# The first half's condition step in two quarters, loads in the order of need, and four engine orders rewritten, in a one-core attention and feed-forward kernel

## The chip, the cores and the metric

The kernel runs on one core of a Trainium2 chip. The metric is device time in microseconds (us) of one execution. The kernel before takes 228.81 us (median of three runs, 228.77 to 230.34). A core has TensorE (PE in the profile, PEld its weight loads), VectorE (DVE), ScalarE (ACT), GpSimd (POOL) and SyncE (SP), each with its own instruction stream; they meet at semaphores only. DMA transfers are issued here from SP and ACT.

## What is computed

`x` is 32 batches x 32 tokens x 256 features. The reference, cut to what matters:

```python
w = cond_weights[itok]                       # (B, 32, 32), one of 8 tables for each batch
c = einsum('bct,bcd->bdt', x, w) + fside[itok][:, :, None]       # the condition step
q, k, v = split(c @ W_qkv + b_qkv)           # 16 heads of 16, causal, scale 1/16
x = x + (softmax(q k^T / 16) v) @ W_out + b_out
g = silu(lora(x, Wg, Ag, Bg)) * lora(x, Wu, Au, Bu)    # adapters Ag[itok], Bg[itok], ...
y = lora(g, Wd, Ad, Bd)
x = x + fwht(silu(y @ W1.T) * (y @ W3.T)) @ W2.T       # Walsh-Hadamard over 1024
```

Products that need it are exact to fp32 by splitting: each operand is hi (rounded to the fast fp32r format) plus lo (the rest), and three matmuls hi*hi, lo*hi, hi*lo are added in PSUM.

## The kernel before, in words

The 1024 tokens are worked in two halves of 512 (s = 0, 1; 16 batches each). 128 feature rows make a chunk c or m. Every engine's order of work is written out by hand as a list of calls, and the PSUM bank of every early tile stands in the table `EARLY_BANKS`.

- **Condition step.** DVE turns the batch indices into one-hots (`index_f`, L866; `onehot_slot`, L869; `onehot_n`, L872). For each half it then multiplies the eight tables by the one-hot (`condition_product`, L877, 1024 elements per partition, written over spare room in `k_x`), adds over the eight (`condition_sum`, L883) and spreads the result block-diagonally over four batches (`condition_blocks`, L889, written over spare room in `prob`). PE multiplies `x_slot` (it lies in `k_x` too) with these blocks, four groups a half and chunk, each of one matmul that the profile shows as two (`conditioned`, L404), and adds the bias rows (`conditioned_bias`, L411), which DVE made (`condition_bias`, L899). The bank `xc` then holds the input of q, k and v.
- ACT rounds it to `act_hi` (`conditioned_hi`, L664), DVE subtracts to get `act_lo` (`conditioned_lo`, L911), and PE forms q, k (`projected`, six matmuls of 512 columns each, L385, L387, L389), v (twelve of 256 columns, L440 to L442), scores (a causal tile, L450, and 64 small matmuls, L460), values (64 small ones, L485), then the output projection, the adapters, gate and up.
- **Softmax, a tile of 512 at a time** (four tiles a half): DVE `maxima`, `less_maxima`; ACT `exps`; DVE `sums`, `inverses`; POOL `normalised` (L1159); DVE `turn` (transpose); ACT `spread_slots`; POOL `spread_first` (L1165). `values(s, 0)` needs tiles 0 and 1, `values(s, 1)` tiles 2 and 3.
- **Weights** come as 25 batches (W_Q, W_K, W_V, W_OUT, W_A, W_GU ...) through a raw buffer of three places. ACT rounds each (`split_weights`, L659), DVE (the first three) or POOL (L1134) makes the rest (`weights_lo`). SP may load a batch into a place only when the batch three earlier has been split.
- `w2_t` (1 MB) lands in `tmp_b`; its four parts are split by ACT (`fold_raw_hi`, L745) and POOL, and PE applies part of the Hadamard transform to it (`fold`, L469).
- At the start PE runs 14 matmuls on zeros (L533).

The order around the change: SP issues const, W_Q, W_K, W_V, matrices, `w2_t`, the residual input (`x_feat`, 1 MB) and then W_OUT and so on. ACT issues the index and the two halves of `x_slots`. PE does the condition step of both halves before anything else.

Of the kernel before, what the change touches and what calls it, by code (L numbers as in the profile page):

```python
# [37 lines left out]
ALU = mybir.AluOpType  # L38
ACT = mybir.ActivationFunctionType
AX = mybir.AxisListType  # L40

P = 128
# [50 lines left out]
def ring_places():  # L93
# [38 lines left out]
def psum_tiles():  # L132
# [7 lines left out]
    plan += [(name, (5, 4, 6, 3, 1, 7, 2, 0)[n % 8]) for n, name in enumerate(later)]  # L140
# [29 lines left out]
def build(nc, index, first, x_slots, w_stream, matrices, w2_t, x_feat, out):  # L170
    with ExitStack() as ctx:
# [10 lines left out]
        index_f = sb("index_f", [P, NG + B])  # L182
# [54 lines left out]
        idx_slot = index_f[:, 0:NG]  # L237
        idx_row = index_f[:, NG:NG + B]
# [103 lines left out]
        def _(sp):  # L342
# [23 lines left out]
        def _(pe):  # L366
# [175 lines left out]
            query(0, 0)  # L542
            key(0, 0)
            fold(0)
            key(0, 1)
            query(0, 1)
            scores(0, 0)
            key(1, 0)
            scores(0, 1)
            query(1, 0)  # L550
            key(1, 1)
            v(0, 0)
            scores(1, 0)
            fold(1)
            v(0, 1)
            query(1, 1)
            values(0, 0)
            v(1, 0)
            scores(1, 1)
            values(0, 1)  # L560
            fold(2)
            project(0, 0, 0, 1)
            v(1, 1)
            project(0, 1, 0)
            project(0, 1, 1)
            fold(3)
            values(1, 0)
            adapters_in(0, 0, 0, 1)
            adapters_in(0, 1, 0)
            gate_up(0, 0)  # L570
# [6 lines left out]
            gate_up_adapters(2, 0)  # L577
            project(1, 0, 0, 1)
            gate_up(3, 0)
            project(1, 1, 0)  # L580
            gate_up_adapters(3, 0)
            project(1, 1, 1)
            gate_up(4, 0)
# [65 lines left out]
        def _(act):  # L649
# [101 lines left out]
            fold_raw_hi(0, 1, 2)  # L751
            conditioned_hi(0, 1)
            fold_raw_hi(3)
            conditioned_hi(1, 0)
            split_weights(W_V)
            conditioned_hi(1, 1)
            split_weights(W_OUT)
            queries(0, 0)
            keys(0, 0, 0, 1)
            evacuate_fold(0)  # L760
            keys(0, 1, 0, 1)
            split_weights(W_A)
            queries(0, 1)
            split_weights(W_GU)
            exps(0, 0)
            keys(1, 0, 0, 1)
            exps(0, 1)
            keys(1, 0, 2, 3)
            exps(0, 2)
            queries(1, 0)  # L770
            keys(1, 1, 0, 1)
            spread_slots(0, 0)
            exps(0, 3)
            evacuate_v(0, 0)
            spread_slots(0, 1)
            keys(1, 1, 2, 3)
            evacuate_v(0, 1)
            spread_slots(0, 2)
            evacuate_fold(1)
            exps(1, 0)  # L780
            even_heads(0, 0)
            queries(1, 1)
            even_heads(0, 1)
            spread_slots(0, 3)
            exps(1, 1)
            attention_hi(0, 0)
            evacuate_v(1, 0)
            spread_slots(1, 0)
            even_heads(0, 2, 3)
            evacuate_fold(2)  # L790
            attention_hi(0, 1)
            spread_slots(1, 1)
# [530 lines left out]
```

## Time and profile before

| | |
|---|---|
| median of 3 runs | 228.81 us (228.77 to 230.34) |
| the profiled execution | 228.75 us, its span 227.0 us |
| busy PE / PEld | 221.5 us (98%) / 179.7 us (79%) |
| busy DVE / ACT / POOL | 84.8 / 100.8 / 121.2 us |
| granted PE clock | full in every slice |
| chain of work that ended last | PE 94%, DVE 3%, DMA 1% |

The span runs from the first instruction to the last; 1.75 us of the execution's own time lie outside it. Matmuls are pipelined, so their busy times overlap and the step from one start to the next tells what one costs.

### The profile page before, as it was taken

To read this page: it belongs to the slowest core of one execution; us is meant where nothing else is said; L and a number is where in the kernel's file an instruction comes from. 1 tells how busy PE (TensorE), PEld (TensorE's weight loads), DVE (VectorE), ACT (ScalarE), POOL (GpSimd) and SP (SyncE) were. 2 spreads that over 40 slices of the span, in tenths; PEclk is the share of its full clock that TensorE was granted. 3 is DMA by queue.
4 is the path that set the end of the run, shared out by engine and by line. 5 is a ranking of instruction groups with operands and counts; after the bars stand their busy time and mean duration, and the time that the engine had idled before them with its cause. 6 is when DMAs were issued, how large, how long until landed. Compare 5 with 4: busy or idle time off the path is not lost.

```text
span 227.0 us, 3701 instructions
## 1 busy us (share of the span) xinstructions
PE 221.5 (98%) x1482; PEld 179.7 (79%) x1482; DVE 84.8 (37%) x141; ACT 100.8 (44%) x169; POOL 121.2 (53%) x93
## 2 busy tenths in 40 slices
PE   7799999999999999999999999999999999999995
PEld 2477787878788888888888888888888888888894
DVE  4988988888454342211022000202222222220211
ACT  2389798895853414756143000313355555440000
POOL 1029676637787297999993800180266667443000
PEclk9999999999999999999999999999999999999999
DMA  6956400004024100330110000031101100000211
GB/s 180 411 212 183 141 1 4 4 3 133 5 72 108 56 0 1 92 92 26 46 46 0 0 3 0 0 92 47 46 3 51 43 0 0 4 0 0 79 62 46
DMA packets 5345, 13.02 MB, mean 57 GB/s; under 512 B 720, under 2 KB 1360, under 8 KB 5072
## 3 DMA queue, kind: packets, MB, share of 16 engines
q1 hardware_dynamic: 4896, 11.72, 16.4%
q10 hardware_dynamic: 432, 1.07, 1.4%
q8 instruction: 12, 0.20, 0.4%
q14 instruction: 5, 0.04, 0.1%
HBM read 11.73 MB, written 1.05 MB: 56 GB/s over the span
## 4 chain that ended last, share of the span: by engine, by line
PE 94%; DVE 3%; DMA 1%; issue 0%; DVEq 0%
PE bank L385 28%; PE bank L389 28%; PE bank L387 28%; PE bank L460 3%; PE bank L485 2%; DMA index_i<-index 1%; DVE cond_sel L883 1%; DVE k_x L877 1%; PE bank L440 1%; PE bank L404 1%; PE bank L441 1%; PE bank L442 1%; PE bank L450 1%; PE bank L469 1%; PE bank L411 0%
## 5 line engine op out<-in xcount | busy, mean ns | idle before, releaser
L1172 POOL TENSOR_TENSOR h_lo<-tmp_b,h_hi 128x512 fp32r<-128x512 f32 x32 | 40.8, 1290 | 30.5 <-ACT h_hi L724 26.3
L385 PE MATMUL bank<-act_hi,w_hi 128*128 128x512 f32 x152 | 52.8, 392 | 0.1
L389 PE MATMUL bank<-act_hi,w_lo 128*128 128x512 f32 x152 | 52.4, 389 | 0.0
L387 PE MATMUL bank<-act_lo,w_hi 128*128 128x512 f32 x152 | 52.3, 389 | 0.0
L1018 DVE TENSOR_TENSOR tmp_b<-bank,tmp_a 128x512 f32<-128x512 f32 x32 | 21.1, 688 | 73.6 <-PE bank L389 56.2
L1134 POOL TENSOR_TENSOR w_lo<-raw,w_hi 128x512 fp32r<-128x512 f32 (+3 forms) x22 | 35.3, 1616 | 10.5 <-ACT w_hi L659 10.5
L385 PEld LDWEIGHTS bank<-act_hi,w_hi 128*128 128x128 f32 x152 | 28.5, 188 | 7.1 <-issue 1.1
L389 PEld LDWEIGHTS bank<-act_hi,w_lo 128*128 128x128 f32 x152 | 28.5, 188 | 6.0
L387 PEld LDWEIGHTS bank<-act_lo,w_hi 128*128 128x128 f32 x152 | 28.5, 188 | 5.7
L724 ACT ACTIVATE h_hi<-tmp_b 128x512 fp32r<-128x512 f32 x32 | 19.8, 632 | 28.4 <-DVE tmp_b L1018 28.4
L385 PE MATMUL bank<-h_hi,w_hi 128*128 128x512 f32 (+1 forms) x88 | 27.3, 370 | 0.0
L389 PE MATMUL bank<-h_hi,w_lo 128*128 128x512 f32 (+1 forms) x88 | 27.3, 370 | 0.0
L387 PE MATMUL bank<-h_lo,w_hi 128*128 128x512 f32 (+1 forms) x88 | 27.3, 370 | 0.0
L734 ACT ACTIVATE tmp_a<-bank 128x512 f32<-128x512 f32 x32 | 18.0, 595 | 20.7 <-PE bank L389 20.7
L659 ACT ACTIVATE w_hi<-raw 128x512 fp32r<-128x512 f32 (+3 forms) x25 | 18.1, 733 | 5.3 <-DMA raw<-w_stream 5.3
L385 PEld LDWEIGHTS bank<-h_hi,w_hi 128*128 128x128 f32 x88 | 16.6, 188 | 2.9
L387 PEld LDWEIGHTS bank<-h_lo,w_hi 128*128 128x128 f32 x88 | 16.6, 188 | 2.8
L389 PEld LDWEIGHTS bank<-h_hi,w_lo 128*128 128x128 f32 x88 | 16.6, 188 | 2.8
L385 PE MATMUL bank<-aux_hi,w_hi 128*128 128x512 f32 x44 | 16.3, 393 | 0.0
L387 PE MATMUL bank<-aux_lo,w_hi 128*128 128x512 f32 x44 | 16.2, 390 | 0.0
L389 PE MATMUL bank<-aux_hi,w_lo 128*128 128x512 f32 x44 | 16.2, 390 | 0.0
L1153 POOL TENSOR_TENSOR w_fold<-w_fold 128x1024 f32<-128x1024 f32 x6 | 15.3, 2561 | 0.0
(85 smaller groups left out, 246.1 us busy)
## 6 DMA issues: line engine op xcount, KB each, us to landing
raw<-w_stream SPq DMA_DIRECT2D x13, 256.0 KB, 2.7
raw<-w_stream SPq DMA_DIRECT2D x8, 384.0 KB, 3.2
raw<-w_stream SPq DMA_DIRECT2D x3, 512.0 KB, 3.6
k_x<-x_slots ACTq DMA_DIRECT2D x2, 512.0 KB, 6.7
tmp_b<-w_t SPq DMA_DIRECT2D x1, 1024.0 KB, 9.0
resid<-x_feat SPq DMA_DIRECT2D x1, 1024.0 KB, 10.9
out_feat<-tmp_b SPq DMA_DIRECT2D x3, 256.0 KB, 2.1
out_feat<-tmp_b SPq DMA_DIRECT2D x2, 128.0 KB, 1.8
```

The source lines that it names most:

```text
L385: pe.matmul(ps[:, :], w[0], x_hi, start=start, stop=False)
L387: pe.matmul(ps[:, :], w[0], x_lo, start=False, stop=False)
L389: last.append(pe.matmul(ps[:, :], w[1], x_hi, start=False, stop=stop))
L460: last = pe.matmul(tiles[i][32 * j:32 * j + 32, g * 4 * T:(g + 1) * 4 * T], q_t[s][q, c, b * T:(b + 1) * T], k_x[s][q, c, b], start=False, ...
L485: last = pe.matmul(o, v_tok[s][rows_, g, c * P + 32 * i:c * P + 32 * i + 32], prob_t[s][rows_, QUADS * c + i // 2, at:at + 2].rearrange("p ...
L659: act.activation(w_hi[:, at:at + COLS[n]], raw[:, n % STAGES, 0:COLS[n]], ACT.Copy)\
L724: act.activation(dst, tmp_b[:, ORDINAL[name, s, m] % 4, :], ACT.Copy).then_inc(prod_hi_made, 1)
L734: free(act.activation(tmp_a[:, n % 4, :], tile(name, s, m)[:, :], ACT.Silu), name, s, m)
L1018: free(dve.tensor_tensor(tmp_b[:, ORDINAL[name, s, m] % 4, :], tile(name, s, m)[:, :], tmp_a[:, silus % 4, :], ALU.mult), name, s, m)
L1134: pool.tensor_tensor(w_lo[:, at:at + COLS[n]], raw[:, n % STAGES, 0:COLS[n]], f32(w_hi[:, at:at + COLS[n]]), ALU.subtract).then_inc(w_lo_m ...
L1153: pool.tensor_tensor(b[:, t], a[:, 0], a[:, 1], ALU.subtract if t else ALU.add)\
L1172: pool.tensor_tensor(lo, tmp_b[:, n % 4, :], f32(hi), ALU.subtract).then_inc(prod_split, 1)
```

## The change

Half 0's condition step is done in two quarters of two groups each: DVE makes product, sum and blocks of each quarter, and PE may start on the first quarter's blocks (`conditioned` now does two groups for half 0, `conditioned_rest` the others). The cast of all 40 indices to fp32 is gone: `onehot_slot` compares the int32 index as it landed, and only the 32 indices of `idx_row` are cast, after it. SP waits for half 0 of `x_slots` before it issues W_V and the matrices, and for half 1 before `w2_t` and the residual input. Half 1's condition step moves behind half 0's q, k and first scores. `k_bias` moves ahead (`key_bias`). The lists of all four engines and the bank table are rewritten to fit. No matmul is added or taken away.

```diff
@@ sync
-            for n in range(STAGES):
-                load_weights(n)
+            load_weights(W_Q)
+            load_weights(W_K)
+            sp.wait_ge(x_loaded[0], 16)
+            load_weights(W_V)
             sp.dma_start(matrix[:, :], matrices).then_inc(matrix_loaded, 16)
+            sp.wait_ge(x_loaded[1], 16)
             sp.dma_start(tmp_b[:, :, :], w2_t.rearrange("p (j n) -> p j n", j=4)).then_inc(w2_loaded, 16)
@@ tensor
             def conditioned(s, c):
                 ps = claim("xc", s, c)
-                pe.wait_ge(blk_made, s + 1)
+                pe.wait_ge(blk_made, 3 if s else 1)
                 pe.wait_ge(x_loaded[s], 16)
-                for g in range(GROUPS):
+                for g in range(GROUPS if s else GROUPS // 2):
...
+            def conditioned_rest(s, c):
+                pe.wait_ge(blk_made, 2)
+                for g in range(GROUPS // 2, GROUPS):
+                    pe.matmul(tile("xc", s, c)[:, g * P:(g + 1) * P], x_slot[s][:, g, c * P:(c + 1) * P],
+                              cond_blk[:, s * GROUPS + g], start=False, stop=False, skip_group_check=True)
...
             conditioned(0, 0)
+            conditioned(0, 1)
+            conditioned_rest(0, 0)
+            conditioned_rest(0, 1)
             conditioned_bias(0, 0)
-            conditioned(0, 1)
             conditioned_bias(0, 1)
+            key(0, 0)
+            query(0, 0)
+            key(0, 1)
+            query(0, 1)
+            scores(0, 0)
             conditioned(1, 0)
+            fold(0)
             conditioned(1, 1)
...
@@ vector
-            dve.tensor_copy(index_f[:, :], index_i[:, :]).then_inc(setup, 1)
             dve.wait_ge(const_loaded, 16)
-            dve.wait_ge(setup, 1)
-            dve.tensor_tensor(onehot_slot[:, :, :], idx_slot.unsqueeze(2).to_broadcast([P, NG, N]),
+            dve.tensor_tensor(onehot_slot[:, :, :], index_i[:, 0:NG].unsqueeze(2).to_broadcast([P, NG, N]),
                               const[:, C_NROW:C_NROW + N].unsqueeze(1).to_broadcast([P, NG, N]),
                               ALU.is_equal).then_inc(setup, 1)
...
+            dve.tensor_copy(idx_row, index_i[:, NG:NG + B]).then_inc(setup, 1)
...
-            condition_product(0)
-            condition_sum(0)
-            condition_blocks(0)
+            condition_product(0, 0)
+            batch_onehots()
+            condition_sum(0, 0)
+            condition_product(0, 1)
+            condition_blocks(0, 0)
+            condition_sum(0, 1)
+            condition_blocks(0, 1)
             condition_bias(0)
```

How the rows stand on the engines that matter. On DVE at the start (`k_x` here is the product, `prob` the blocks, `w_hi` and `w_lo` of 8 partitions the bias rows), before:

```order
L866 CAST index_f<-index_i 128x40
L869 TENSOR_TENSOR onehot_slot<-index_f,const 128x64
L872 TENSOR_SCALAR onehot_n<-index_f,const 128x32
L877 TENSOR_TENSOR k_x<-const,onehot_slot 128x1024
L883 TENSOR_REDUCE cond_sel<-k_x 128x128
L889 TENSOR_TENSOR prob<-cond_sel,const 128x512
L899 TENSOR_TENSOR w_hi<-onehot_n,fs_hi 8x512
L899 TENSOR_TENSOR w_lo<-onehot_n,fs_lo 8x512
L877 TENSOR_TENSOR k_x<-const,onehot_slot 128x1024
```

and with the change:

```order
L874 TENSOR_TENSOR onehot_slot<-index_i,const 128x64
L877 CAST idx_row<-index_i 128x32
L891 TENSOR_TENSOR k_x<-const,onehot_slot 128x512
L881 TENSOR_SCALAR onehot_n<-idx_row,const 128x32
L899 TENSOR_REDUCE cond_sel<-k_x 128x64
L891 TENSOR_TENSOR k_x<-const,onehot_slot 128x512
L906 TENSOR_TENSOR prob<-cond_sel,const 128x256
L899 TENSOR_REDUCE cond_sel<-k_x 128x64
L906 TENSOR_TENSOR prob<-cond_sel,const 128x256
L916 TENSOR_TENSOR w_hi<-onehot_n,fs_hi 8x512
L916 TENSOR_TENSOR w_lo<-onehot_n,fs_lo 8x512
L923 TENSOR_TENSOR w_lo<-raw,w_hi 128x512 x2
```

The first blocks come after half-size steps, and the rest of W_Q and W_K now comes before half 1's product instead of after half 1's whole step.

On ACT from the first weight split on, with the change (`w_hi<-tmp_b` is a part of `w2_t`, the `w_hi<-raw` between the two `q_t` rows is W_OUT, the next one W_A):

```order
L668 ACTIVATE w_hi<-raw 128x512 x2
L673 ACTIVATE act_hi<-bank 128x512 x2
L668 ACTIVATE w_hi<-raw 128x512
L684 ACTIVATE k_x<-bank,k_bias,const 128x16x32 x2
L754 ACTIVATE w_hi<-tmp_b 128x512 x2
L677 ACTIVATE q_t<-bank,const 128x512
L668 ACTIVATE w_hi<-raw 128x512
L677 ACTIVATE q_t<-bank,const 128x512
L754 ACTIVATE w_hi<-tmp_b 128x512
L668 ACTIVATE w_hi<-raw 128x512
L754 ACTIVATE w_hi<-tmp_b 128x512
L684 ACTIVATE k_x<-bank,k_bias,const 128x16x32 x2
```

W_OUT, W_A and all of `w2_t` now stand ahead of half 0's second keys, which `scores(0, 1)` needs.

On POOL, the softmax of half 0 (`prob` is `normalised`, `k_x` is `spread_first`), before:

```order
L1134 TENSOR_TENSOR w_lo<-raw,w_hi 128x768
L1159 TENSOR_TENSOR prob<-prob,row_inv 128x512 x3
L1165 TENSOR_TENSOR k_x<-k_x,const 128x16x32
L1159 TENSOR_TENSOR prob<-prob,row_inv 128x512
L1165 TENSOR_TENSOR k_x<-k_x,const 128x16x32 x2
L1159 TENSOR_TENSOR prob<-prob,row_inv 128x512
L1165 TENSOR_TENSOR k_x<-k_x,const 128x16x32
```

and with the change:

```order
L1155 TENSOR_TENSOR w_lo<-raw,w_hi 128x768
L1180 TENSOR_TENSOR prob<-prob,row_inv 128x512 x4
L1186 TENSOR_TENSOR k_x<-k_x,const 128x16x32 x4
L1180 TENSOR_TENSOR prob<-prob,row_inv 128x512 x2
L1155 TENSOR_TENSOR w_lo<-raw,w_hi 128x768
```

All eight steps of half 0 now stand together, ahead of half 1's first.

## Rows read from the trace of the kernel before

**Rows 1.** The page: busy time (us, share, instructions).

```profile
PE 221.5 (98%) x1482; PEld 179.7 (79%) x1482; DVE 84.8 (37%) x141; ACT 100.8 (44%) x169; POOL 121.2 (53%) x93
```

**Rows 2.** Waits of PE after the warm-up (us in total, times, longest).

```profile
PE bank L404 <- DVE prob L889: 1.4, 2, 0.8
```

**Rows 3.** The chain that ended last, 0 to 48.3 us (start, us, what).

```profile
0.74 2.65 DMA index_i<-index
3.41 0.20 DVE index_f L866
...
3.71 0.23 DVE onehot_slot L869
3.93 0.15 DVE onehot_n L872
4.08 1.14 DVE k_x L877
5.25 1.23 DVE cond_sel L883
...
11.55 2.05 PE bank L404 x16
13.61 1.12 PE bank L411 x4
14.73 0.43 PE bank L385
...
18.17 0.23 PE bank L385
...
21.34 1.49 PE bank L460 x64
...
48.18 0.10 issue
```

**Rows 4.** Timeline (start, us, what; in brackets the idle time before and its releaser).

```profile
1.19 5.26 PE L533 MATMUL bank<-warm 128*128 128x512 bf16 x14 [1.19 <-DVE warm L864]
6.50 0.69 DVE L889 TENSOR_TENSOR prob<-cond_sel,const 128x512 f32<-128x512 f32 x1
7.11 0.67 DVE L899 TENSOR_TENSOR w_hi<-onehot_n,fs_hi 8x512 fp32r<-8x512 f32 x1
7.71 0.67 DVE L899 TENSOR_TENSOR w_lo<-onehot_n,fs_lo 8x512 fp32r<-8x512 f32 x1
7.25 1.16 PE L404 MATMUL bank<-prob,k_x 128*128 128x128 f32 x8 [0.79 <-DVE prob L889]
```

**Rows 5.** Timeline at 14 to 15.5 us: how ACT, DVE and PE hand over.

```profile
14.00 0.57 ACT L664 ACTIVATE act_hi<-bank 128x512 fp32r<-128x512 f32 x1
14.61 0.69 DVE L911 TENSOR_TENSOR act_lo<-bank,act_hi 128x512 fp32r<-128x512 f32 x1 [0.71 <-ACT act_hi L664]
15.35 0.19 PEld L385 LDWEIGHTS bank<-act_hi,w_hi 128*128 128x128 f32 x1 [0.16 <-DVE act_lo L911]
```

**Rows 6.** Loads: their issue in the timeline, and us to landing.

```profile
1.16 0.95 ACTq L652 DMA_DIRECT2D k_x<-x_slots  x2
DMA to landing us min/median/max: 5.9/6.7/7.5
resid<-x_feat SPq DMA_DIRECT2D x1, 1024.0 KB, 10.9
8.48 0.63 ACT L659 ACTIVATE w_hi<-raw 128x512 fp32r<-128x512 f32 x1 [1.71 <-DMA raw<-w_stream]
13.32 12.30 SPq L348 DMA_DIRECT2D raw<-w_stream  x6
```

**Rows 7.** Timeline: `scores(0, 1)` on PE, the last `spread_first` of half 0, and `values(0, 1)`.

```profile
24.80 1.56 PE L460 MATMUL bank<-k_x,q_t 64*32 64x128 f32 x64
39.37 1.04 POOL L1165 TENSOR_TENSOR k_x<-k_x,const 128x512 f32<-128x512 f32 x1 [0.18 <-ACT k_x L697]
40.61 1.15 PE L485 MATMUL bank<-k_x,v_tok 64*32 64x128 f32 x64
```

More of the change, by code:

```diff
@@ L139, in psum_tiles @@
     later += [("w2", j, 0) for j in range(len(OUTS))]
-    plan += [(name, (5, 4, 6, 3, 1, 7, 2, 0)[n % 8]) for n, name in enumerate(later)]
+    plan += [(name, (4, 2, 3, 1, 7, 6, 5, 0)[n % 8]) for n, name in enumerate(later)]
     held = [0] * 8
@@ L541, in _ @@
             conditioned_bias(1, 1)
[L542 to L547, printed above, removed]
+            scores(0, 1)
             key(1, 0)
-            scores(0, 1)
             query(1, 0)
+            v(0, 0)
             key(1, 1)
-            v(0, 0)
+            v(0, 1)
             scores(1, 0)
+            v(1, 0)
+            values(0, 0)
             fold(1)
-            v(0, 1)
+            values(0, 1)
             query(1, 1)
-            values(0, 0)
-            v(1, 0)
-            scores(1, 1)
[L560 to L566, printed above, removed]
+            v(1, 1)
+            project(0, 0, 0, 1)
+            fold(2)
+            project(0, 1, 0)
+            fold(3)
+            project(0, 1, 1)
+            scores(1, 1)
+            adapters_in(0, 0, 0, 1)
+            gate_up(0, 0)
+            adapters_in(0, 1, 0)
             values(1, 0)
-            adapters_in(0, 0, 0, 1)
-            adapters_in(0, 1, 0)
-            gate_up(0, 0)
             adapters_in(0, 1, 1)
@@ L750, in _ @@
             conditioned_hi(0, 0)
-            fold_raw_hi(0, 1, 2)
             conditioned_hi(0, 1)
+            split_weights(W_V)
+            keys(0, 0, 0, 1)
+            fold_raw_hi(0, 1)
+            queries(0, 0)
+            split_weights(W_OUT)
+            queries(0, 1)
+            fold_raw_hi(2)
+            split_weights(W_A)
             fold_raw_hi(3)
+            keys(0, 1, 0, 1)
+            exps(0, 0)
+            evacuate_fold(0)
             conditioned_hi(1, 0)
-            split_weights(W_V)
@@ L756, in _ @@
             conditioned_hi(1, 1)
[L757 to L763, printed above, removed]
+            exps(0, 1)
             split_weights(W_GU)
-            exps(0, 0)
             keys(1, 0, 0, 1)
-            exps(0, 1)
+            exps(0, 2)
             keys(1, 0, 2, 3)
-            exps(0, 2)
+            exps(0, 3)
             queries(1, 0)
+            spread_slots(0, 0)
@@ L785, in _ @@
-            exps(1, 1)
-            attention_hi(0, 0)
+            exps(1, 1)
+            even_heads(0, 1)
+            evacuate_fold(1)
+            even_heads(0, 2, 3)
+            attention_hi(0, 0)
+            queries(1, 1)
+            attention_hi(0, 1)
+            keys(1, 1, 2, 3)
+            split_weights(W_GU + 1)
+            evacuate_fold(2)
+            evacuate_fold(3)
+            residual_hi(0, 0)
+            split_weights(W_GU + 2)
+            residual_hi(0, 1)
+            spread_slots(1, 0)
@@ new lines, in groups, with condition_product @@
+            def groups(s, quarter):
+                half_ = GROUPS // 2
+                return range(GROUPS) if quarter is None else range(quarter * half_, (quarter + 1) * half_)
+            def condition_product(s, quarter=None):
+                gs = groups(s, quarter)
+                dve.wait_ge(setup, 1)
+                dve.tensor_tensor(cond_prod[s][:, gs.start:gs.stop],
+                                  cond_all.unsqueeze(1).to_broadcast([P, len(gs), T, N]),
+                                  onehot_slot[:, s * GROUPS + gs.start:s * GROUPS + gs.stop, :].unsqueeze(2)
+                                  .to_broadcast([P, len(gs), T, N]), ALU.mult).then_inc(prod_cond, 1)
@@ new lines, in condition_sum, with condition_blocks @@
+            def condition_sum(s, quarter=None):
+                gs = groups(s, quarter)
+                dve.wait_ge(prod_cond, 3 if s else quarter + 1)
+                dve.tensor_reduce(cond_sel[:, s * GROUPS + gs.start:s * GROUPS + gs.stop],
+                                  cond_prod[s][:, gs.start:gs.stop], AX.X, ALU.add).then_inc(sel_made, 1)
+            def condition_blocks(s, quarter=None):
+                gs = groups(s, quarter)
+                g = slice(s * GROUPS + gs.start, s * GROUPS + gs.stop)
+                dve.wait_ge(sel_made, 3 if s else quarter + 1)
@@ L1028, in _ @@
+            conditioned_lo(0, 1)
             condition_product(1)
+            key_bias()
+            condition_bias(1)
+            constants()
+            keys(0, 0, 2, 3)
             condition_sum(1)
             condition_blocks(1)
-            condition_bias(1)
-            weights_lo(W_Q)
-            conditioned_lo(0, 0)
-            conditioned_lo(0, 1)
-            weights_lo(W_K)
-            constants()
             weights_lo(W_V)
+            maxima(0, 0, 1)
+            less_maxima(0, 0)
```

159 lines of the change are left out of this document (63 added, 96 removed), and 24 rows, old and new, of the table EARLY_BANKS.

## The prediction

> **What bounds the kernel now.** I read the page's busy times first: PE is busy 98% of the span [rows 1], so only time in which PE stands idle or does needless work can be won. The waits view says where it stands: after the warm-up PE waits for one thing, the blocks of the condition step, twice and 1.4 us in all [rows 2], and for nothing else in the whole execution, apart from a break of 0.10 us at 48.18 [rows 3]. The chain of waits shows the same start: the index lands at 3.39, then comes an unbroken run of DVE steps (cast, one-hots, product, sum, blocks, bias rows, and the same again for half 1), and from 11.55 on the chain is PE alone [rows 3]. So the whole stake lies before 11.55. The timeline prices it. PE's first useful matmul starts at 7.25 [rows 4]. One half's condition work is 2.05 + 1.12 = 3.17 us of PE (16 and 4 matmul records, [rows 3]); half 0's would end at 7.25 + 3.17 = 10.42 and half 1's blocks come at 11.55, so 1.13 us are lost after the start. The warm-up ends at 1.19 + 5.26 = 6.45 [rows 4]; it is unchanged, and nothing useful can precede it. The most that can be won is therefore (7.25 - 6.45) + 1.13 + 0.10 = 2.0 us, or 0.9% of 228.75. A change of this kernel under 1% is what I call "the same".
>
> **The first blocks.** Before, they are ready at 6.50 + 0.69 = 7.19 [rows 4]. With the change the one-hot starts when the index has landed, 3.41, as the cast did. I have no row of a compare on int32; I take the fp32 row's 0.23 [rows 3] (bounds: the same row, or the cast's 0.20 on top, 0.43). The cast of 32 indices costs 0.15, between nothing and the 0.20 of the cast of 40. Halves of 1024-element steps: two steps of 512 start 0.60 apart (7.11, 7.71 [rows 4]), and a full one takes 1.14 to 1.23 [rows 3], so splitting costs nothing where steps follow without a dependence, and up to the 0.07 between 0.60 and 0.67 where one waits for the one before. So: product from 3.80, `onehot_n` 0.15, sum of the first quarter at 4.56 (it waits for its product), product of the second to 5.77, then blocks of 256 elements; their row is missing, between 0.35 (half the 0.69) and 0.69, I take 0.42: ready at **6.20**. The second quarter's blocks: 5.77 + 0.35 + 0.70 + 0.42 = 7.26. The bias rows follow, 0.60 and 0.67: 8.46, against 8.38 before [rows 4]. The saving of the first blocks is 1.0 us. A rule speaks against the split: the Trainium skill, "VectorE: DVE Perf Modes", section on the trn2 errata, says that each instruction on SBUF data pays a fixed latency and advises tiles of at least 512 elements; three more instructions at about 150 cycles of 0.96 GHz would put the bias rows at about 8.9, an estimate by that page. That would still change nothing in the sum below, but it would take about 0.3 us off the gain of the first rival.
>
> **But `x_slots` also has to be there.** Half 0's transfer is issued at 1.16 and takes 5.9 us: it lands at 7.06 [rows 6], hidden before behind blocks of 7.19. It now ends the wait: PE starts at about **7.1**, not 6.45. Whether it comes sooner when SP holds W_V back is the main doubt. W_K lands at about 8.45 (ACT's split starts at 8.48 after waiting for it [rows 6]), later than `x_slots`, and W_V stands behind W_K on SP's queue, so I take no gain; the bound is all that the warm-up allows, 0.6 us. The Trainium skill, "DMA: Bandwidth & Descriptors", section "Queues, rings and completion order", says that each DMA engine consumes one ring's descriptors in order and alternates between rings; by it W_V took next to nothing from `x_slots` before 7.06, and the sum is the one with no gain.
>
> From 7.1 the four quarters (two chunks each) are the same 16 records, 2.05: 9.16, later than the 8.46 of the bias rows and with both quarters' blocks long there. The bias for both chunks is 1.12: 10.28. Then PE has nothing to cover the hand-over, where before it had half 1. Chunk 0's bias ends at about 9.9; ACT starts `act_hi` at 9.93, DVE follows 0.61 later and PE 0.74 after that (14.00, 14.61, 15.35 [rows 5]): the first key starts at 9.93 + 0.61 + 0.74 = **11.28**. This adds a wait of 1.0 us. W_Q's and W_K's rests on DVE end at 8.46 + 0.60 + 0.67 = 9.7, in time for it. Chunk 1 follows 0.6 behind and is needed 0.7 behind. Before, q began at 14.73 with both halves' conditions done [rows 3]; half 1's 3.17 now come later, so the like figure is 11.28 + 3.17 = 14.45. **Net gain at the start: 14.73 - 14.45 = 0.28 us.** Of the 1.93 that PE lost, 1.65 stays, in other places.
>
> **The rewritten middle.** Here PE waited for nothing, so the best it can do is nothing. I walked the four lists with the rows' durations: 0.23 a matmul and 1.49 for scores [rows 3], about 0.6 a DVE or ACT step [rows 4, 5], 1.04 a POOL step [rows 7].
> - `conditioned(1, ...)` comes after four projections (24 x 0.23) and scores with their causal tiles (0.45 + 1.49): 11.28 + 5.5 + 0.1 + 1.94 = 18.8. Its blocks, behind 0.1 of `key_bias`, bias rows, constants and half of the keys on DVE, come at about 18.5. Slack 0.3.
> - W_OUT is split on ACT ahead of `queries(0, 1)`. SP waits for half 1's `x_slots` (1.16 + 0.46 + 7.5 = 9.1 before [rows 6], by the rate about 8.2 now), then sends 2 MB. Before, the residual input landed at 3.92 + 10.9 = 14.8 [rows 6]; now I put it about 0.6 later and W_OUT 0.6 behind that, at 16.1. The chain from W_OUT over q, the rest of `w2_t`, W_A, two keys on ACT and two on DVE is 5.6 us, and PE wants the end of it at 22.95: slack 1.2.
> - `values(0, 1)`: PE is there at 36.4 (`scores(0, 1)` ends at 24.45, then 18 x 0.23, three v parts of 1.44, scores 1.94, values 1.09 and fold 0.46). The fourth `inverses` of half 0 comes at 30.8 by the walk, then POOL has five steps of 1.03: 35.9. Slack 0.5.
> - `project(0, 0)` wants its input at 40.3, and DVE gives it at 40.2. Slack 0.1, the least of all.
>
> After that every slack is 0.3 or more, and from `gate_up` on the work is what it was. The break of 0.10 at 48.18 goes, since scores(1, 1) now cover that residual. I take no stall in the middle. Sum, against the profiled execution: 228.75 - 0.28 - 0.10 = **228.4 us**; that execution is 0.06 under the median of the runs, so the two bases agree.
>
> **Rivals.**
> 1. *`x_slots` lands sooner.* For it: SP's queue is empty behind W_K until it lands, so what shared bandwidth with it before is less; against it: the order on the queue, above. PE starts when the warm-up lets it, at 6.5, and every step to the first key moves with it (bias rows 8.46 against a need at 8.55): 0.6 more, 227.8 us. Chance 0.22.
> 2. *The softmax of half 0 comes late for `values(0, 1)`, and the kernel is slower.* Before, the last `spread_first` ends at 39.37 + 1.04 = 40.41, which is 14.05 after `scores(0, 1)` ended (24.80 + 1.56 [rows 7]), and PE came 0.2 later, at 40.61. Now PE comes 11.95 after. If the chain over DVE, ACT and POOL takes as long as before, PE waits 2.1 us: 230.5 us. It decides from 36.4 on. Against it: POOL's eight steps stand together and it stood idle before most of them. For it: DVE and ACT hold two more condition steps in that stretch. Chance 0.13, with part of the price as likely as all of it.
> 3. *W_OUT lands after 17.3* because the gated queue leaves bandwidth unused. ACT works in order, so q, keys and `scores(0, 1)` wait with it, one for one. At 18.3: 229.4 us. Chance 0.07.
> 4. *The change does not do what it says:* `x_slots` lands later, or PE's new wait of 1.0 us is longer by the 0.3 that was won, or `project(0, 0)` is 0.3 late. 228.7 to 229.0 us. Chance 0.08.
>
> The forecast keeps 0.50, with 228.1 to 228.7 as its own range. 8 in 10 lie between **227.6 and 229.7**: rival 1 is inside, rival 2 up to a third of its way or a bit more, rivals 3 and 4 inside. More than 1% faster (226.5) is beyond the most that can be won, 0.02 for errors of the trace; more than 1% slower (231.1) needs rival 2 and another together, 0.05; the same 0.93.
>
> **What would show it.** The first useful matmul at 7.1, released by the load and not by DVE (6.5 for rival 1; a release by the blocks would refute the 6.20). A wait of PE of about 1.0 us for `act_lo` of chunk 0, the first key at 11.3. Half 1's condition at 18.8 and `values(0, 1)` at 36.4 without a wait; a wait there for POOL is rival 2, one of ACT for W_OUT's load followed by one of PE ahead of `scores(0, 1)` rival 3. The granted clock should stay full. I am wrong if PE waits over 0.5 us after 12 us, if `gate_up` of both halves is touched at all, or if the start is won by more than 0.9 us.

## The result, and the profile after

The changed kernel takes 232.46 us (median of six runs, 230.59 to 234.84) against 228.78 us for the kernel before (six runs, 228.74 to 230.34). The ratio is 1.0132, 95% interval 1.0098 to 1.0166: it is slower by 1.3%, outside the range of 227.6 to 229.7. That is also more than the 1% up to which the prediction would call it the same. A run more than 1.5% above the fastest run of its kernel counts as slow and is left out of the ratios (here 234.84; the other five have a median of 232.03), while every median and range given is that of all runs. The profiled execution took 232.89 us with a span of 231.1 us, 4.14 us more than the profiled one before.

The first lines of the page of the changed kernel, to be held against [rows 1] (busy us, share, instructions; `PEclk` in tenths, 40 slices):

```profile
span 231.1 us, 3699 instructions
PE 223.0 (97%) x1478; PEld 180.9 (78%) x1482; DVE 89.5 (39%) x144; ACT 100.7 (44%) x169; POOL 121.1 (52%) x93
PEclk9979999999999999999999999999999999999999
```

PE has the same matmuls (the page lists four records fewer, 1478 for 1482, but as many weight loads). DVE has 4.7 us more of busy time for three more small instructions, and the clock has a dent in the third slice. Now the waits of PE, which answer to [rows 2] (us in total, times, longest):

```profile
PE bank L386 <- DVE aux_lo L1030: 1.9, 1, 1.9
...
PE bank L386 <- DVE act_lo L928: 1.0, 1, 1.0
PE bank L386 <- issue: 0.4, 1, 0.4
PE bank L405 <- DMA k_x<-x_slots: 0.4, 1, 0.4
PE bank L467 <- DVE k_x L949: 0.2, 1, 0.2
```

The two waits for `prob` of [rows 2] are gone. In their place stand the two that were forecast (`x_slots`, 0.4, and `act_lo`, 1.0), and one of 1.9 us that was not forecast, far behind the rewritten part. The start, against [rows 4] and [rows 5], from the timeline (start, us, what; in brackets the idle time before and its releaser):

```profile
5.62 0.41 DVE L906 TENSOR_TENSOR prob<-cond_sel,const 128x256 f32<-128x256 f32 x1
6.66 0.42 DVE L906 TENSOR_TENSOR prob<-cond_sel,const 128x256 f32<-128x256 f32 x1
6.96 1.13 PE L405 MATMUL bank<-prob,k_x 128*128 128x128 f32 x8 [0.37 <-DMA k_x<-x_slots]
9.67 1.08 ACT L673 ACTIVATE act_hi<-bank 128x512 fp32r<-128x512 f32 x2 [0.78 <-PE bank L418]
10.30 1.29 DVE L928 TENSOR_TENSOR act_lo<-bank,act_hi 128x512 fp32r<-128x512 f32 x2 [0.69 <-ACT act_hi L673]
11.14 0.47 PE L386 MATMUL bank<-act_hi,w_hi 128*128 128x512 f32 x1 [1.04 <-DVE act_lo L928]
```

Blocks at 6.03 (forecast 6.20), PE's start at 6.96 released by the load (7.1), the wait for the first key 1.04 (1.0), the first key at 11.14 (11.28). The start is right to 0.2 us. Then three things go wrong, one behind the other.

**The clock falls.** Stretches of the execution by windows (PE, PEld, DVE, ACT, POOL busy with instructions, then PEclk, DMA share, GB/s):

```profile
12.60:15.90 3.30, 3.30 (x9) 2.54 (x8) 3.30 (x10) 1.89 (x3) 0.00 (x0) 0.50 0.96 392
16.00:17.00 1.00, 1.00 (x6) 0.81 (x5) 1.00 (x2) 1.00 (x3) 0.77 (x1) 1.00 0.86 328
```

Here PE is never idle and has a granted clock of 0.50, which is 1.2 GHz instead of 2.4; 3.41 us after it fell (12.52) it is full again. A matmul of 512 columns steps 0.43 in there instead of 0.23, and about 1.5 us are lost. Before the fall lie the two idle stretches of the new start, 0.37 us up to 6.96 and 1.04 us up to 11.14 (the brackets above). They do not always bring it: two of the six runs of this kernel, 232.03 and 231.63 us, kept a full clock.

**W_OUT is late.** SP's issues, against the row of SPq in [rows 6], and then the chain that ended last up to `scores(0, 1)` (start, us, what):

```profile
1.18 5.99 SPq L346 DMA_DIRECT2D raw<-w_stream  x3
...
8.73 0.33 SPq L355 DMA_DIRECT2D tmp_b<-w_t  x1
9.10 0.43 SPq L356 DMA_DIRECT2D resid<-x_feat  x1
9.57 10.55 SPq L346 DMA_DIRECT2D raw<-w_stream  x3
```

```profile
9.57 9.22 DMA raw<-w_stream
...
18.82 0.63 ACT w_hi L668
...
19.93 0.62 ACT w_hi L754
20.55 0.52 ACT w_hi L668
21.07 0.52 ACT w_hi L754
21.59 1.34 ACT k_x L684 x2
...
23.02 1.54 DVE k_x L949 x2
...
24.70 1.56 PE bank L467 x64
```

W_OUT lands at 18.80, 2.7 us after the 16.1 of the forecast. `w2_t` (issued at 8.73, 6.7 us to landing) came at 15.4 and the residual input (9.10, 9.0 us) at 18.1. The chain from W_OUT to `scores(0, 1)` is 5.88 us long; it was put at 5.6. Why so late shows in the transfer rates, before:

```profile
7.00:9.00 2.00, 1.63 (x10) 1.26 (x10) 2.00 (x4) 0.52 (x1) 0.00 (x0) 1.00 1.06 415
9.00:12.00 3.00, 2.42 (x15) 1.71 (x15) 2.93 (x4) 0.71 (x2) 0.00 (x0) 1.00 1.01 428
```

and after:

```profile
7.00:9.00 2.00, 2.00 (x17) 1.88 (x17) 1.96 (x5) 0.63 (x1) 0.00 (x0) 1.00 0.75 246
9.00:12.00 3.00, 1.96 (x8) 1.33 (x9) 2.31 (x4) 1.60 (x3) 0.00 (x0) 1.00 0.83 257
10.00:10.50 0.50, 0.10 (x1) 0.00 (x0) 0.20 (x1) 0.50 (x2) 0.00 (x0) 1.00 0.25 66
```

In these five microseconds (415 - 246) x 2 + (428 - 257) x 3 = 851 KB less were moved, 2.0 us at 420 GB/s. Without the gates (experiment 1) the same two windows move 418 and 429 GB/s, so the loss belongs to the gates. The last row shows the price of issuing late: `w2_t` was issued at 8.73, and from 10.00 to 10.50 the rate is still only 66 GB/s (360 before).

How both meet at `scores(0, 1)`: before, it began at 24.80 [rows 7] with the six matmuls of `key(1, 0)` ahead of it, which now come later; without their 1.37 us (an estimate, six steps of 0.23) that is 23.43. Now it begins at 24.70, **1.27 us late** instead of 0.28 early. The clock brings PE to its place at about 24.5 anyway, and the load holds it 0.17 longer: two causes beside each other, of which in this execution either alone would have cost most of it. The load varies: in experiment 2, with the same gates, W_OUT was split at 17.94, and without a fall of the clock `scores(0, 1)` was only 0.39 late.

**A step of VectorE is held for 2.2 us.** The adapters of half 1. After:

```profile
84.67 2.37 POOL L1174 TENSOR_TENSOR w_fold<-w_fold 128x1024 f32<-128x1024 f32 x1
84.68 2.92 DVE L1030 TENSOR_TENSOR aux_lo<-tmp_b,aux_hi 128x512 fp32r<-128x512 f32 x1 [0.70 <-ACT aux_hi L733]
87.74 0.47 PE L386 MATMUL bank<-aux_hi,w_hi 128*128 128x512 f32 x1 [1.87 <-DVE aux_lo L1030]
```

and the same place before:

```profile
82.72 0.69 DVE L1011 TENSOR_TENSOR aux_lo<-tmp_b,aux_hi 128x512 fp32r<-128x512 f32 x1 [0.70 <-ACT aux_hi L724]
82.74 2.92 POOL L1153 TENSOR_TENSOR w_fold<-w_fold 128x1024 f32<-128x1024 f32 x1
83.75 0.39 PE L385 MATMUL bank<-aux_hi,w_hi 128*128 128x512 f32 x1
```

The DVE step is the same, 512 elements, 0.69 before and 2.92 now. POOL does two folding steps (`butterflies`) there, and the rows show the second. After, it began at 84.67, a few ns ahead of DVE, and took 2.37; DVE ended 0.55 behind it. Before, DVE began 0.02 ahead and kept its 0.69, and the fold took 2.92. So, as far as the records can tell a few ns, whichever starts first runs, and the other stands still until it is done. The seven profiles that have this meeting agree: in the changed kernel and experiments 1, 2 and 5 the two start within 0.01 us of each other and DVE takes 2.90 to 2.93; in the kernel before and experiments 6 and 7 the fold starts 0.02 later and DVE takes 0.69. The Trainium skill, "SBUF — State Buffer", section "Who interferes with whom", states that a DVE instruction with two SBUF inputs contends with a GpSimd instruction that reads SBUF, that the shared port pair is an exclusive lock, and that the order of issue decides who is blocked. The trace agrees, with 0.55 us lost by POOL one way and 2.23 by DVE the other.

These rows also give the account. At 84.68 against 82.72 the program is 1.96 late, at 87.74 against 83.75 it is 3.99: 1.27 at `scores(0, 1)`, 0.7 in the middle, 2.0 by the hold; the last 0.15 up to 4.14 come right behind it.

### The profile page after: what moved, and what is told of

It reads as the page before. It is cut to its first block, busy times and chain, and to the rows that moved or that the text cites. A ratio compares the mean times of both kernels' runs of the same rounds, so it can differ in the third digit from the quotient of the medians.

```text
span 231.1 us, 3699 instructions
## 1 busy us (share of the span) xinstructions
PE 223.0 (97%) x1478; PEld 180.9 (78%) x1482; DVE 89.5 (39%) x144; ACT 100.7 (44%) x169; POOL 121.1 (52%) x93
## 4 chain that ended last, share of the span: by engine, by line
PE 86%; DMA 7%; DVE 3%; ACT 2%; issue 1%; SPq 0%; DVEq 0%
PE bank L386 27%; PE bank L390 26%; PE bank L388 26%; DMA raw<-w_stream 7%; PE bank L467 2%; PE bank L492 2%; DVE aux_lo L1030 1%; PE bank L447 1%; PE bank L448 1%; PE bank L449 1%; ACT w_hi L668 1%; DVE k_x L949 1%; ACT k_x L684 1%; ACT w_hi L754 0%; PE bank L476 0%
## 5 line engine op out<-in xcount | busy, mean ns | idle before, releaser
L386 PE MATMUL bank<-act_hi,w_hi 128*128 128x512 f32 x152 | 53.6, 398 | 1.4 <-DVE act_lo L928 1.0
L388 PE MATMUL bank<-act_lo,w_hi 128*128 128x512 f32 x152 | 53.0, 393 | 0.0
L1155 POOL TENSOR_TENSOR w_lo<-raw,w_hi 128x512 fp32r<-128x512 f32 (+3 forms) x22 | 36.1, 1645 | 11.5 <-ACT w_hi L668 11.5
L390 PEld LDWEIGHTS bank<-act_hi,w_lo 128*128 128x128 f32 x152 | 29.0, 190 | 6.2
L388 PEld LDWEIGHTS bank<-act_lo,w_hi 128*128 128x128 f32 x152 | 29.0, 191 | 5.9
L668 ACT ACTIVATE w_hi<-raw 128x512 fp32r<-128x512 f32 (+3 forms) x25 | 18.1, 732 | 6.8 <-DMA raw<-w_stream 6.7
L1174 POOL TENSOR_TENSOR w_fold<-w_fold 128x1024 f32<-128x1024 f32 x6 | 14.7, 2474 | 0.0
```

Source lines behind the costliest of these rows:

```text
L386: pe.matmul(ps[:, :], w[0], x_hi, start=start, stop=False)
L388: pe.matmul(ps[:, :], w[0], x_lo, start=False, stop=False)
L390: last.append(pe.matmul(ps[:, :], w[1], x_hi, start=False, stop=stop))
L668: act.activation(w_hi[:, at:at + COLS[n]], raw[:, n % STAGES, 0:COLS[n]], ACT.Copy)\
L1155: pool.tensor_tensor(w_lo[:, at:at + COLS[n]], raw[:, n % STAGES, 0:COLS[n]], f32(w_hi[:, at:at + COLS[n]]), ALU.subtract).then_inc(w_lo_m ...
L1174: pool.tensor_tensor(b[:, t], a[:, 0], a[:, 1], ALU.subtract if t else ALU.add)\
```

## The experiments

Four theories stand in the expectations. **G**: the gates on SP's queue make W_OUT late, and ACT, in order, hands that on. **C**: idle stretches of PE make the granted clock fall. **P**: a DVE step and a POOL step hold each other, and their order within some ns decides which. **F**: the sequencer of PE runs dry behind a long run of small matmuls (the 0.4 us on "issue" above). The kernel before, run beside them, took 228.8 us in each of the three groups of runs (medians of 19, 31 and 29), 230.2 to 230.5 in those of its executions whose mean clock was 0.993 (7, 5 and 7 of them), and 228.7 to 229.7 in the others.

**1. No gates.**

```diff
             load_weights(W_K)
-            sp.wait_ge(x_loaded[0], 16)
             load_weights(W_V)
             sp.dma_start(matrix[:, :], matrices).then_inc(matrix_loaded, 16)
-            sp.wait_ge(x_loaded[1], 16)
```

> The changed kernel without SP's two waits for x_slots; all else stays. Theory G (the gates): held back, w2_t, the residual input and W_OUT land late (W_OUT at 18.8 instead of about 16), and ACT, in order, delays the second q and keys of half 0, so that scores(0, 1) starts at 24.70. Without the gates W_OUT lands at about 16 and the wait ahead of scores(0, 1) goes: 0.4 us less if the clock falls as in the changed kernel's profile (PE comes late then anyway), up to 1.8 us less if it does not. Theory C (the clock): no change beyond 0.4 us, since the slow stretch at 12.5 to 15.9 us is still there. Theory P (VectorE and GpSimd hold each other): no effect but by chance, the wait of 1.9 us at 87.7 comes or goes with the nanoseconds.

Measured: 231.53 us (231.19 to 233.09, four runs), ratio 1.0127 (1.0072 to 1.0182). The timeline, ACT's split of W_OUT and PE:

```profile
15.81 0.63 ACT L666 ACTIVATE w_hi<-raw 128x512 fp32r<-128x512 f32 x1
...
23.14 1.13 PE L465 MATMUL bank<-k_x,q_t 64*32 64x128 f32 x48 [0.23 <-DVE k_x L947]
```

W_OUT is split 3.0 us sooner and `scores(0, 1)` begins at 23.14, 0.29 before the like point of the kernel before: the gain that was forecast for the start is there. This execution also kept its clock (mean 0.999), although PE stood idle for 1.19 and 1.04 us at the start, so G and C are not parted by it, and idle time does not always bring the fall. PE's wait of 1.9 us for `aux_lo` stays, and with it most of the loss. The time as a whole says little for G: the ratios with and without gates are 1.0132 and 1.0127, and among runs at full clock it is 231.63 and 232.03 with the gates against 231.19, 231.37 and 231.69 without, some 0.4 us.

**2. Gates kept, PE's gap filled.**

```diff
+            for _ in range(4):
+                pe.matmul(banks[7][:, :], warm[:, 0:P], warm[:, :], start=True, stop=True)
             key(0, 0)
```

> The changed kernel with four more matmuls on zeros (512 columns each, about 0.85 us) in PE's gap between the bias of the condition step and the first key. Theory C: the clock fell at 12.5 us because PE stood idle before; with the gap filled the granted clock stays full, the first four projections end 1.5 us sooner. Theory G: most of these 1.5 us then turn into a wait ahead of scores(0, 1), which stays at about 24.7, so the time gains under 0.4 us. If C alone were right, the kernel would gain 1.5 us.

Measured: 234.22 us (233.19 to 234.75, four runs), ratio 1.0219 (1.0176 to 1.0261), slower than the change itself. Two stretches by windows:

```profile
12.00:15.00 3.00, 3.00 (x15) 2.49 (x14) 3.00 (x9) 1.89 (x3) 0.00 (x0) 1.00 0.98 404
24.00:30.00 6.00, 6.00 (x72) 4.86 (x66) 5.40 (x11) 1.79 (x4) 3.31 (x3) 0.50 0.41 121
```

and, between them, `scores(0, 1)` in the timeline:

```profile
23.82 1.08 PE L467 MATMUL bank<-k_x,q_t 64*32 64x128 f32 x16 [0.91 <-DVE k_x L951]
```

The fall at 12.5 is gone, as C says. But PE, now in time, meets the keys of the late W_OUT (split at 17.94 here) and waits 0.91, and there the clock falls, for 6.83 us. This is G alone: 0.39 late at `scores(0, 1)`, and the wait then costs more by the clock than by itself. Here the filled gap only moved the fall to the next idle place; all four runs have a mean clock of 0.985 or 0.993. The expected gain (up to 0.4 us) did not come.

**3. POOL's folds one place later.**

```diff
-                if m < 3:
-                    butterflies(m, 0)
-                    butterflies(m, 1)
+                if 1 <= m < 4:
+                    butterflies(m - 1, 0)
+                    butterflies(m - 1, 1)
```

> The changed kernel with POOL's six Hadamard steps on w2 (butterflies) one place later in its list, behind the next hidden_lo and weight split. Theory P: the wait of 1.9 us ahead of the adapters of half 1 is a VectorE subtraction that started 6 ns after a butterfly and was held until that ended; moved, it takes 0.7 us again and the kernel gains 1.9 us in the executions that had it. Theories G and C: nothing changes.

Measured: 230.62 us (228.91 to 233.11, ten runs), ratio 1.0047 (1.0007 to 1.0087). The same DVE step:

```profile
84.78 0.69 DVE L1030 TENSOR_TENSOR aux_lo<-tmp_b,aux_hi 128x512 fp32r<-128x512 f32 x1 [0.70 <-ACT aux_hi L733]
```

0.69 again, no wait of PE there, and a span of 229.0 instead of 231.1: P is worth 2.1 us of the profiled execution. The clock fell at 11.45 in it for 3.41 us, and `scores(0, 1)` began at 24.98. Of the ten runs the two at full clock took 228.91 and 229.32, against 232.03 and 231.63 for the changed kernel at full clock: the hold is its largest loss. The eight others have a lower clock: four took 230.15 to 230.83, and four 231.12 to 233.11, which no profile explains.

**4. All three.**

> The changed kernel with all three edits: no gates, the gap filled, butterflies later. If G, C and P are the whole loss, it loses the 1.5 us of the clock, the 0.4 us of waits ahead of scores(0, 1) and the 1.9 us at the adapters: about 3.8 us under the changed kernel, 228.6 us, no slower than the kernel before. If something else is at work, it stays above 229.5 us.

Measured: 229.42 us (228.97 to 229.92, ten runs), ratio 1.0015 (0.9996 to 1.0034), all at full clock. That is 0.8 us above the 228.6 expected and just under the 229.5 that would have meant something else at work. Behind the start PE's waits are one of 0.6 us on "issue" and two of 0.2. The first of them, in the timeline:

```profile
38.99 0.41 PE L490 MATMUL bank<-k_x,v_tok 64*32 64x128 f32 x4 [0.58 <-issue]
```

`scores(0, 1)` begins at 23.24, 0.19 early. So G, C and P together explain most of the loss: by the medians 3.0 of 3.7 us, by the ratios (1.0132 to 1.0015) 2.7 of 3.0. What is left arises between 24 and 84 us. The profiled execution is the slowest of the ten (229.92) and is 1.13 us late at the adapters (`aux_lo` at 83.85 instead of 82.72); the largest piece is the break of 0.58 in the middle of `values(0, 1)`, for which the trace shows no releaser.

**5. Gates and filling kept, W_OUT and W_A issued ahead of the residual input.**

```diff
             sp.dma_start(tmp_b[:, :, :], w2_t.rearrange("p (j n) -> p j n", j=4)).then_inc(w2_loaded, 16)
+            load_weights(W_OUT)
+            load_weights(W_A)
             sp.dma_start(resid[:, :, :], x_feat).then_inc(resid_loaded, 16)
...
-            for n in range(STAGES, BATCHES):
+            for n in range(W_GU, BATCHES):
```

> The changed kernel with the filled gap (four matmuls on zeros ahead of the first key) and the gates kept, but SP issues W_OUT and W_A ahead of the residual input instead of behind it. To be held against the run with the filled gap alone, where PE waited 1.3 us at scores(0, 1) and the clock then fell for 6.8 us. Theory G: W_OUT behind 2 MB is the cause; now it lands before 17, scores(0, 1) starts at 23.2 instead of 23.8, the wait shrinks to the 0.3 us of VectorE's keys, the clock stays full and the time falls by 2.5 to 3.5 us, to about 231.3. If the gates act in another way (w2_t late, say), W_OUT's place changes little. The wait of 1.9 us at the adapters stays, since the Hadamard steps are not moved.

Measured: 231.73 us (229.41 to 235.03, ten runs), ratio 1.0070 (1.0030 to 1.0111), 2.5 us less than experiment 2 by the medians, from the order of two loads. ACT splits W_OUT at 16.68 instead of 17.94 and no longer waits for it. But the start of `scores(0, 1)` is not the expected 23.2:

```profile
18.84 1.76 DVE L927 TENSOR_TENSOR w_lo<-raw,w_hi 128x512 fp32r<-128x512 f32 x1
23.97 1.24 PE L469 MATMUL bank<-k_x,q_t 64*32 64x128 f32 x52 [0.81 <-DVE k_x L953]
```

It is 0.15 later than in experiment 2 (where PE waited 0.91; the 1.3 of the expectation is DVE's wait for ACT there), since now DVE is behind: POOL holds two of its steps ahead of the keys, this one of 1.76 and the blocks of half 1 (1.53). The wait of 0.81 brought no fall of the clock here. So the gain is not a shorter wait; it stands in the clock, full in eight of ten runs and in none of four of experiment 2. Why the clock held in most of them, with a wait nearly as long, is not shown. Its runs at full clock fall into two groups, four at 229.41 to 230.08 and four at 231.52 to 232.22. The profiled one had the hold (a DVE step of 2.9 at 83.76), and behind PE's wait of 1.9 the clock fell, as this stretch by windows shows (in the changed kernel and experiments 1 and 2 the same wait brought no fall):

```profile
88.00:91.00 3.00, 3.00 (x9) 2.33 (x8) 0.69 (x1) 1.70 (x3) 0.55 (x1) 0.50 0.00 0
```

**6. The kernel before, its gaps filled.**

```diff
-WARM_UP = 14
+WARM_UP = 17
...
+            for _ in range(2):
+                pe.matmul(banks[7][:, :], warm[:, 0:P], warm[:, :], start=True, stop=True)
             conditioned(1, 0)
```

> The kernel before with three more matmuls on zeros in its warm-up (17 instead of 14) and two more in PE's gap before the condition step of half 1; both stand where PE waited. Theory C: about a third of the executions of the kernel before are 1.55 us longer, with a mean granted clock of 0.993, because the clock falls after these gaps; with the gaps filled every execution shows a full clock and 228.8 us, give or take 0.1. If the fall has another cause, a third of the executions stay at 230.3.

Measured: 228.81 us (228.68 to 229.10, eleven runs), ratio 0.9992 (0.9974 to 1.0010), with a mean clock of 0.999 or more in all eleven. The kernel before has the 230.3 us in 19 of the 79 executions beside these experiments. At that rate none in eleven would come by chance once in twenty times, so this supports C without settling it by itself. The median is that of the kernel before.

**7. The quarters and the compare of the int32 index alone, in the kernel before.** No order and no load is changed but that of the condition step; its edit on DVE, in part:

```diff
-            condition_product(0)
-            condition_sum(0)
-            condition_blocks(0)
+            condition_product(0, 0)
+            batch_onehots()
+            condition_sum(0, 0)
+            condition_product(0, 1)
...
```

> The kernel before with one part of the change alone: half 0's condition step in quarters and the index compared as int32; loads and all orders as before. By the forecast's sum the first useful matmul comes at 7.0 instead of 7.25 (the load of x_slots bounds it), but half 1's blocks still come from VectorE at about 11.6, so that the gain is nothing: 228.8 us at full clock, and a PE gap before 11.6 that is longer by 0.3 us, which can only make the clock fall more often. If the quarters were worth their whole 1.0 us, it would be 228.0.

Measured: 228.93 us (228.67 to 233.35, ten runs), ratio 1.0019 (0.9995 to 1.0044).

```profile
5.70 0.41 DVE L905 TENSOR_TENSOR prob<-cond_sel,const 128x256 f32<-128x256 f32 x1
7.23 1.13 PE L402 MATMUL bank<-prob,k_x 128*128 128x128 f32 x8 [1.48 <-DVE prob L905]
```

Blocks at 6.11, yet PE starts at 7.23 as before (7.25). The view names `prob` as the releaser, but that had been done for a microsecond: it is `x_slots`, whose wait stands beside it in `conditioned` and which lands 5.9 us after its issue at 1.16. Half 1's blocks come at 11.53 instead of 11.55. The part of the change that looks like the gain gives nothing by itself; four of its ten runs had the lower clock (the profiled one, at full clock, has gaps of 1.48 and 1.14 us).

**8. All three, and two more edits:** `weights_lo(W_V)` on DVE ahead of half of the keys, and `query(1, 1)` on PE ahead of `values(0, 1)`.

> The changed kernel with the gates off, the gap filled, the Hadamard steps one place later (as in the run with all three), and two more edits: VectorE makes the rest of W_V ahead of half 0's keys instead of at 18.1 us, where a GpSimd step held it for 1.1 us, and PE does query(1, 1) between the two values of half 0, since PE stood for 0.6 us without any wait inside the second, after two bursts of 64 small matmuls close together (theory F: it runs out of fetched instructions). If P and F hold, scores(0, 1) starts 0.3 us sooner and the break of 0.6 us is gone: 228.4 to 228.7 us, 0.8 us under the run with all three. If F is wrong, the break moves with the second values and the gain is 0.3 us at most.

Measured: 230.25 us (229.92 to 230.96, nine runs), ratio 1.0063 (1.0045 to 1.0081); 0.8 us worse than experiment 4. The expectation was wrong. The step that POOL held was `w_lo` of W_V, which nobody needed soon. With it moved, POOL holds the blocks of half 1, on which PE waits:

```profile
17.38 1.30 POOL L1155 TENSOR_TENSOR w_lo<-raw,w_hi 128x512 fp32r<-128x512 f32 x1
17.63 1.60 DVE L906 TENSOR_TENSOR prob<-cond_sel,const 128x512 f32<-128x512 f32 x1
19.33 0.35 PE L403 MATMUL bank<-prob,k_x 128*128 128x128 f32 x1 [0.85 <-issue]
```

The blocks took 0.72 in experiment 4 and 1.60 here: P once more, now on the path. The break on "issue" did not go either; it is 0.70 us, at 42.27.

**9. Experiment 5 and the later folds.**

> The change with both waits of SP kept, four more zero matmuls, W_OUT and W_A issued ahead of the residual input, and the weight folds (butterflies) of GpSimd one place later. It differs from out_first, 229.4 to 232.2 us at full clock, by the folds alone. Theory P (a VectorE step and a GpSimd step hold each other when they start within some ns, here at the adapters of half 1): the upper group of runs (231.5 to 232.2) disappears, the one long wait of PE for aux_lo (1.9 us) with it, and the runs gather at 229.2 to 230.0. Rival (the two groups come from something else, as the clock alone): the groups stay 2 us apart.

Measured: 229.54 us (228.90 to 232.27, twelve runs), ratio 1.0017 (0.9987 to 1.0048). The upper group is gone: eleven of twelve runs lie at 228.90 to 230.20 (the twelfth, 232.27, has a mean clock of 0.985), and no wait for `aux_lo` is left. So the two groups of experiment 5 were the hold, there in some executions and not in others of one and the same program. `scores(0, 1)` begins at 23.64. With the gates kept and the two loads ahead, the time is that of having no gates (229.42), though the gates still show: ACT waits 1.77 us for `w2_t`, and PE 0.55 us for `q_t`.

**10. The kernel before with the later folds.**

> The kernel before with the weight folds of GpSimd one place later, as in late_fold. Control of theory P: in the kernel before PE never waits for aux_lo, so there is no hold to take away: 228.8 us, within 0.3, and 230.3 in executions whose clock falls once. Rival (later folds are worth 2 us by themselves, through GpSimd's load): 227 us or less, or slower if the folded weights then come late.

Measured: 228.80 us (228.67 to 230.40, twelve runs), ratio 0.9992 (0.9972 to 1.0013). One run of the twelve had the lower clock. Later folds are worth nothing where nothing was held on the path. So P is the meeting of the two steps, not POOL's load.

**11. Experiment 4 with `query(1, 1)` ahead of `values(0, 1)`.**

> As all_three (229.42 us), with one PE entry moved: query(1, 1), whose matmuls are 512 columns wide, goes between values(0, 1) and what stood ahead of it. No instruction is added or taken away. Theory F (PE ran out of fetched instructions after a long run of small matmuls, 0.58 us without any wait): the break in values(0, 1) goes or shrinks to under 0.2, 228.8 to 229.1 us. Rival (the break belongs to the place in the program and not to the small matmuls): it stays at 0.4 to 0.6 us, 229.4 us.

Measured: 229.80 us (229.56 to 230.09, twelve runs), ratio 1.0023 (1.0002 to 1.0043). PE's timeline:

```profile
38.48 1.16 PE L490 MATMUL bank<-k_x,v_tok 64*32 64x128 f32 x64
40.98 0.28 PE L447 MATMUL bank<-w_hi,act_lo 128*128 128x256 f32 x1
41.97 0.47 PE L384 MATMUL bank<-aux_hi,w_hi 128*128 128x512 f32 x1 [0.71 <-issue]
```

`values(0, 1)` runs without a break, but one of 0.71 has come three microseconds later, ahead of `project(0, 0)`. Neither F nor its rival as written: the break moved and did not go. Whether it is the fetching of instructions stays open.

## Why the prediction was wrong

- **The first blocks, `x_slots`, the hand-over, the first key: right.** 6.03, 6.96, a wait of 1.04, 11.14. The net gain of 0.28 at the start shows as 0.29 in experiment 1 and 0.19 in experiment 4. That the quarters alone would win nothing is experiment 7. Rival 1 is refuted: PE starts at 6.96 with W_V held back and at 6.95 without (experiment 1). Two smaller readings were off, and nothing came of them: 5.77 + 0.35 + 0.70 + 0.42 is 7.24, which puts the bias rows at 8.51 and not 8.46, and the end of the warm-up is not fixed at 6.45, since the same 14 matmuls end at 1.19 + 4.53 = 5.72 in experiment 10.
- **"W_OUT ... at 16.1 ... slack 1.2": the step that failed first.** It landed at 18.80. The residual input was put "about 0.6 later" than before, as if a queue that is opened late only shifts by the wait. In truth neither `w2_t` nor the residual input moved at all before the issues at 8.73 and 9.10, and their 2 MB took until 18.1. Rival 3 named the mechanism and its point (17.3) and priced it at 1 us with a chance of 0.07. Experiments 1 and 2 show it: without the gates ACT splits W_OUT 3.0 us sooner, and with them PE waits 0.91 us ahead of `scores(0, 1)` even at full clock. By itself this costs little, 0.39 us there and some 0.4 us between runs at full clock; more comes of it only where the clock falls behind the wait.
- **"The granted clock should stay full": wrong.** It was taken from a profile of the kernel before in which the clock is full in every slice. The text did count PE's new wait of 1.0 us, but as 1.0 us only. With the fall behind it that microsecond of idleness costs 2.5, and four of the six runs of the changed kernel had it. The times given of the kernel before already held the sign of it, 230.34 beside 228.77 and 228.81; the like executions beside the experiments have a mean clock of 0.993, which shows that this is the clock, and with filled gaps none of the 21 runs of experiments 4 and 6 had it.
- **"From `gate_up` on the work is what it was": wrong, and the largest term.** The work is the same, its meeting with POOL is not. With everything some 2 us later, a fold of POOL that began 0.02 us behind the DVE step that PE waits for now begins within 0.01 us of it, and holds it. The prediction priced every DVE step from the row of a free one. Experiments 3, 9 and 10 show it: 2.1 us in the profiles, and 2.3 to 3.1 us between the runs at full clock (231.63 and 232.03 against 228.91 and 229.32). The trace of before had such steps, as these rows of DVE and POOL (a like step of DVE took 0.75 when free), and they were passed over:

```profile
56.14 1.54 DVE L972 SCALAR_TENSOR_TENSOR aux_lo<-q_t,const,aux_hi 128x512 fp32r<-128x512 f32 x1
55.66 1.47 POOL L1159 TENSOR_TENSOR prob<-prob,row_inv 128x512 f32<-128x512 f32 x1 [1.38 <-DVE row_inv L955]
```

- **"I take no stall in the middle": nearly.** `values(0, 1)` began at 38.71 without a wait, its inputs from POOL done at 33.86 + 4.03 = 37.89: rival 2 is false. It is so with PE on time too: in experiment 4 POOL was done at 36.46 and PE came at 37.29. PE's own way there was walked 0.6 us too short, 13.45 us from the start of `scores(0, 1)` against 14.01 and 14.05 measured, so that at the forecast 36.4 PE would have stood on the edge of a wait. The break at 48.18 gave way to one of 0.39 at 40.25. With G, C and P taken out, some 0.6 us of loss remain by the medians (experiments 4 and 9, both intervals reach to no difference). Breaks of PE are part of it; the other parts are open.
- The sum of 228.4 therefore stood on a right start (-0.3) and left out, in the profiled execution, +1.5 (load and clock together), +0.7 (middle) and +2.1 (hold). The most that could be won was 2.0 us; the loss was not bounded by that.

## What to carry to other kernels

Where PE is 98% busy, a reordering has a couple of microseconds to win and can lose more, since an idle microsecond of PE may bring a stretch at half its clock: fill idle places, and look at the spread of the runs before trusting one profile's full clock. A gate on a load queue costs transfer time as well as the wait, so what an in-order engine needs next goes first behind it. Before moving anything, list the VectorE steps with two SBUF inputs that stand near a long GpSimd step and on which PE waits soon: their price has two values, and any shift can change which one holds.

## What the runs showed of the hardware that was not expected

- The granted clock fell to 0.50 (1.2 GHz) behind idle stretches of PE of 0.9 to 1.9 us, and stayed there with PE fully busy, for 3.41 us in the changed kernel and 6.83 us in experiment 2. One fall of 3.41 us cost about 1.5 us: 230.4 against 228.8 in the kernel before. Not every execution with the same gaps has it: 19 of 79 of the kernel before; and a wait of 1.9 us brought no fall in the profiles of the changed kernel and experiments 1 and 2.
- A DVE step of 0.69 us took 2.92 when a POOL step had begun a few ns before it, and the POOL step 2.92 instead of 2.37 the other way round. DVE steps with an input in PSUM were not held: the 32 of the gated products (`tmp_b<-bank,tmp_a`) took 0.68 to 0.69 each, beside a POOL that was busy for half of the span.
- One program has two times, 2 us apart, which experiment 9 puts down to such a hold: 229.4 to 230.1 and 231.5 to 232.2 us in experiment 5, both at full clock.
- PE broke off for 0.4 to 0.7 us without any wait in the profile, at different places in five kernels (the changed one and experiments 1, 4, 8 and 11). A transfer of 0.02 MB on the instruction queue stands one to three microseconds ahead of each, but every profile has twelve such transfers, and behind the one at 36.7 in the kernel before there is no break at all; behind the one at 36.4 in experiment 9 there is only a slower `values(0, 1)`, 1.53 us instead of 1.16. The cause is open.
